# Mixture of experts in a two-layer decoder: routing and tiles in one stage, tiles of 256 tokens instead of 512

## The reference, cut to what matters

```
scores = sigmoid(x @ router_w.T) + routing_bias          # [4096, 8]
top 2 of the 8 experts, weights normalised by their sum
expert(x) = (silu(x @ wg.T) * (x @ wu.T)) @ wd.T         # wg, wu: [512, 256]; wd: [256, 512]
y = expert_shared(x) + sum over the 2 chosen e of weight_e * expert_e(x)
```

## Time and profile before

| | |
|---|---|
| time, median of 3 runs | 3147.19 us (3143.03 to 3158.15) |
| time of the profiled execution | 3143.8 us |
| its span | 3142.0 us |
| PE, PEld busy | 2614.6 us (83%), 2153.7 us (69%) |
| DVE, ACT, POOL busy | 1964.2 us (63%), 1431.5 us (46%), 1466.5 us (47%) |
| mean granted TensorE clock | 0.901 of 2.4 GHz |

### The profile page before, as it was taken

One profiled execution on the slowest core, in us unless ns is written; L12 is line 12 of the kernel. 1 busy time (PEld: TensorE's weight loads), 2 busy tenths in 40 slices (PEclk: granted clock), 3 DMA queues, 4 the chain that ended last, 5 costly groups with the idle time before them and its releaser, 6 DMA issues. The chain is left out here.

```text
span 3142.0 us, 67197 instructions
## 1 busy us (share of the span) xinstructions
PE 2614.6 (83%) x25004; PEld 2153.7 (69%) x25004; DVE 1964.2 (63%) x3461; ACT 1431.5 (46%) x2236; POOL 1466.5 (47%) x1604
## 2 busy tenths in 40 slices
PE   4999999994999964899999703888885799958998
PEld 3676667763666664788888603777775577747998
DVE  2676666673678714555555575887885377754554
ACT  2565555651566622344444302555552356632332
POOL 3565666653455315622222282444444477743333
PEclk7999999996999967999999956888897799989999
DMA  6565556624777624443434272000001777730111
GB/s 163 131 149 134 140 138 149 142 65 118 203 201 201 154 72 150 169 158 136 165 134 164 95 216 69 28 31 20 30 21 52 184 205 201 198 106 28 44 44 40
DMA packets 253341, 380.48 MB, mean 121 GB/s; under 512 B 53200, under 2 KB 190800, under 8 KB 246736
## 3 DMA queue, kind: packets, MB, share of 16 engines
q1 hardware_dynamic: 239328, 311.01, 37.3%
q0 software_dynamic: 10608, 65.55, 6.1%
q10 hardware_dynamic: 3200, 1.05, 0.2%
HBM read 242.80 MB, written 145.75 MB: 124 GB/s over the span
## 5 line engine op out<-in xcount | busy, mean ns | idle before, releaser
L1225 ACT ACTIVATE self_probs<-self_score_ps 128x768 f32<-128x768 f32 x256 | 207.6, 811 | 219.2 <-PE self_score_ps L1127 216.0
L1433 POOL TENSOR_SCALAR_AFFINE_SELECT self_probs<-self_probs 128x512 f32<-128x512 f32 x256 | 167.5, 655 | 217.5 <-ACT self_probs L1225 214.9
L1354 DVE TENSOR_REDUCE self_neg_max<-self_max_ps 128x2 f32<-128x256 f32 x256 | 108.2, 423 | 229.6 <-PE self_max_ps L1113 225.5
L1976 POOL TENSOR_TENSOR moee_w_lo<-moee_w_in,moee_w_hi 128x1536 fp32r<-128x1536 f32 x31 | 109.5, 3532 | 203.9 <-ACT moee_w_hi L1888 203.8
L672 DVE TENSOR_REDUCE cross_neg_max<-cross_max_ps 128x4 f32<-128x1024 f32 x128 | 155.9, 1222 | 67.0 <-PE cross_max_ps L461 65.8
L1912 DVE TENSOR_TENSOR moee_h<-moee_u_ps,moee_silu 128x512 f32<-128x512 f32 x124 | 85.5, 690 | 152.0 <-PE moee_u_ps L81 150.6
L1873 ACT ACTIVATE moee_h_hi<-moee_h 128x512 fp32r<-128x512 f32 x124 | 78.3, 632 | 221.5 <-DVE moee_h L1912 219.3
L1355 DVE TENSOR_REDUCE self_neg_max<-self_max_ps 128x2 f32<-128x512 f32 x256 | 174.6, 682 | 0.0
L1915 DVE TENSOR_TENSOR moee_h_lo<-moee_h,moee_h_hi 128x512 fp32r<-128x512 f32 x124 | 119.2, 961 | 86.5 <-ACT moee_h_hi L1873 76.0
L589 ACT ACTIVATE cross_probs<-cross_score_ps 128x1024 f32<-128x1024 f32 x128 | 131.1, 1024 | 89.4 <-PE cross_score_ps L483 89.2
L2823 POOL TENSOR_TENSOR ffn_g_lo<-ffn_g_full,ffn_g_hi 128x512 fp32r<-128x512 f32 x64 | 82.3, 1287 | 187.5 <-ACT ffn_g_hi L2747 187.5
(11 more groups left out here) (448 smaller groups left out, 9683.8 us busy)
## 6 DMA issues: line engine op xcount, KB each, us to landing
self_q<-self_q_split SPq DMA_DIRECT2D x48, 512.0 KB, 3.2
self_q_raw<-self_q SPq DMA_DIRECT2D x32, 768.0 KB, 7.9
cross_stacks<-cross_qk SPq DMA_DIRECT2D x64, 384.0 KB, 6.4
causal_stacks<-causal_qk SPq DMA_DIRECT2D x64, 384.0 KB, 6.7
moee_x_t<-x_tiles SPq DMA_DIRECT2D x31, 512.0 KB, 5.4
moe_y_tiles<-moee_y SPq DMA_DIRECT2D x31, 512.0 KB, 4.5
x_tiles<-zeros SPq DMA_DIRECT2D x16, 736.0 KB, 5.1
cross_qk<-cross_k_split SPq DMA_DIRECT2D x16, 512.0 KB, 3.9
```

The source lines that it names most:

```text
L1225: nc.scalar.activation(probs[g % 4][:, a, :, P:], score_ps[:, :, P:], ACT.Exp, scale=HD ** -0.5).then_inc(prob_ready, 1)
L1433: pool.affine_select(diagonal, diagonal, [[0, 2], [0, 2], [1, P]], ALU.is_ge, zero, base=0, channel_multiplier=-1).then_inc(prob_masked, 1)
L1976: pool.tensor_tensor(w_lo[p][:, 0:LO_POOL], w_in[:, 0:LO_POOL], w_hi[p][:, 0:LO_POOL].bitcast(F32), ALU.subtract).then_inc(wlo_ready, 1)
```

## The change

The stages route and expert_tiles become one stage (all names now `moee_`), and the tiles become smaller:

- TILE is 256. There are 16 shared and 39 routed tiles, 55 in all. Two blocks of hidden features make a pair, so that the ACT and DVE instructions on `silu` and `h` stay 512 columns wide; the matmuls of expand are 256 columns wide.
- The shared expert's weights are loaded and split once, while PE still transposes for the router (`scan`). Shared tiles take their tokens from `x_tok` in SBUF.
- Only the choice of experts stands ahead of the first tile on DVE (`choose`); the rest of the routing is put between the instructions of shared tiles 0, 1 and 2 (`weigh`, `count_chunks`, `start_experts`, `place_choices`, `name_tiles`), the two counting matmuls stand after the first tile's expand. The 64 scatters stand in one row on POOL.
- A routed tile's weights come in two indirect DMAs, 1 MB for gate and up (`in_raw`, asked for two tiles ahead) and 0.5 MB for down (`out_raw`, one tile ahead), each into two buffers. DVE writes the low part of half of the first, POOL that of the other half and of the whole second.
- Contract of a tile runs one tile later, between the expands of the next tile.

```diff
-TILE = 512
+TILE = 256
...
+            def rank_choices():
+                pe.wait_ge(both_ready, 1)
+                flat = both[:].rearrange("p c e -> p (c e)")
+                pe.matmul(prefix_ps, before, flat, start=True, stop=True)
+                pe.matmul(total_ps, ones, flat, start=True, stop=True).then_inc(prefix_done, 1)
...
             def body(st):
-                for f in range(WT):
+                for f in range(PAIRS):
+                    if f == 1 and st.has(1):
+                        transpose_x(st)
                     if st.has(0):
                         expand(st, f)
-                    if f == 0 and st.has(-1):
-                        contract(st, -1, WT - 1)
-                    if f > 0 and st.has(0):
-                        contract(st, 0, f - 1)
-                    if f == 0 and st.has(1):
-                        transpose_x(st)
+                    if f == 1 and shared(st) and st.at(0) == 0:
+                        rank_choices()
+                    if st.has(-1):
+                        contract(st, f)
...
+                for f in range(PAIRS):
+                    if f == 0 and fresh(st, 1):
+                        split_in(st)
...
+                    if f == 1 and fresh(st):
+                        split_out(st)
...
+                if fresh(st, 2):
+                    n = st.parity(2)
+                    if fresh(st):
+                        dve.wait_ge(out_loaded[buffer(st)], 16 * turn(st))
+                    dve.tensor_scalar(row[n][:], tile_expert[:, bass.ds(st.at(2), 1)], float(P), part_no,
                                       ALU.mult, ALU.add).then_inc(row_ready, 1)
-                for f in range(WT):
+                if fresh(st, 1):
+                    n = buffer(st, 1)
+                    dve.wait_ge(inhi_ready, sets(st, 1))
+                    dve.tensor_tensor(in_lo[n][:, IN_POOL:], in_raw[n][:, IN_POOL:], in_hi[n][:, IN_POOL:].bitcast(F32),
+                                      ALU.subtract).then_inc(inlo2_ready, 1)
+                for f in range(PAIRS):
+                    if f == 1 and st.has(1):
+                        dve.wait_ge(xhi_ready, st.done(1))
+                        if st.has(-1):
+                            dve.wait_ge(gu_done, 2 * PAIRS * st.done(-1))
+                        dve.tensor_tensor(x_lo[1 - p][:].rearrange("p k s -> p (k s)"), xT_ps[:],
+                                          x_hi[1 - p][:].bitcast(F32).rearrange("p k s -> p (k s)"),
+                                          ALU.subtract).then_inc(xlo_ready, 1)
                     if st.has(0):
...
+                    if f == 0 and st.has(-2):
+                        dve.wait_ge(down_done, PAIRS * st.done(-2))
+                        if st.has(-4):
+                            dve.wait_ge(stored[p], st.nth(-2) * 16)
+                        dve.tensor_copy(y[p][:].rearrange("p q d -> p (q d)"), y_ps[p][:]).then_inc(y_kept, 1)
+                    if shared(st) and st.has(0):
+                        if (st.at(0), f) == (0, 1):
+                            weigh()
+                            found["sums"] = count_chunks()
+                        if (st.at(0), f) == (1, 0):
+                            found["end"] = start_experts(found["sums"])
+                        if (st.at(0), f) == (1, 1):
+                            place_choices(found["sums"])
+                        if (st.at(0), f) == (2, 1):
+                            name_tiles(found["end"])
...
+            pool.wait_ge(inhi_ready, 1)
+            pool.tensor_tensor(in_lo[0][:, 0:IN_POOL], in_raw[0][:, 0:IN_POOL], in_hi[0][:, 0:IN_POOL].bitcast(F32),
+                               ALU.subtract).then_inc(inlo_ready, 1)
+            pool.wait_ge(outhi_ready, 1)
+            pool.tensor_tensor(out_lo[0][:], out_raw[0][:], out_hi[0][:].bitcast(F32),
+                               ALU.subtract).then_inc(outlo_ready, 1)
             pool.wait_ge(prefilled, B * 16)
-            n_scatter = -(-TOP * NT // (SHARED - 1))
+            for k in range(TOP):
+                pool.wait_ge(slot_ready, k + 1)
+                for c in range(NT):
+                    pool.indirect_dma_start(x_tiles, bass.IndirectOffsetOnAxis(ap=slot[k][:, c:c + 1], axis=0),
+                                            x_tok[:, c, :], None).then_inc(scattered, 16)
...
+                        pool.wait_ge(row_ready, sets(st, 2) - 1)
+                        pool.wait_ge(inlo_ready, sets(st))
+                        pool.wait_ge(inlo2_ready, sets(st))
+                    pool.wait_ge(outlo_ready, sets(st, -1))
                     pool.tensor_tensor(gate[:], part_no, part_no, ALU.add).then_inc(gate_set, 1)
-                    pool.indirect_dma_start(w_in[:], None, experts,
+                if fresh(st, 2):
+                    pool.indirect_dma_start(in_raw[buffer(st, 2)][:], None, experts_in,
+                                            bass.IndirectOffsetOnAxis(ap=row[st.parity(2)][:], axis=0)
+                                            ).then_inc(in_loaded[buffer(st, 2)], 16)
+                if fresh(st, 1):
...
+                    pool.indirect_dma_start(out_raw[n][:], None, experts_out,
                                             bass.IndirectOffsetOnAxis(ap=row[st.parity(1)][:], axis=0)
...
+                                            ).then_inc(out_loaded[n], 16)
+                    pool.wait_ge(inhi_ready, sets(st, 1))
+                    pool.tensor_tensor(in_lo[n][:, 0:IN_POOL], in_raw[n][:, 0:IN_POOL],
+                                       in_hi[n][:, 0:IN_POOL].bitcast(F32), ALU.subtract).then_inc(inlo_ready, 1)
+                if fresh(st):
+                    n = buffer(st)
+                    pool.wait_ge(outhi_ready, sets(st))
+                    pool.tensor_tensor(out_lo[n][:], out_raw[n][:], out_hi[n][:].bitcast(F32),
+                                       ALU.subtract).then_inc(outlo_ready, 1)
```

More of the change, by code:

```diff
@@ L1591, in _, with fresh, gate_cols, up_cols @@
+        def fresh(st, d=0):
+            return st.has(d) and not shared(st, d)
+        def gate_cols(t, k, f):
+            return t[:, k * FF + f * P:k * FF + (f + 1) * P]
+        def up_cols(t, k, f):
+            return t[:, (KT + k) * FF + f * P:(KT + k) * FF + (f + 1) * P]
         @block.sync
         def _(sp):
[L1593 to L1594 removed]
+            for dst, src in ((ident[:], consts["ident"]), (rw[:], router), (bias[:], router_bias.partition_broadcast(P)),
+                             (table[:], tables)):
@@ L1600, in _ @@
+            run(sp, body)
+            for p in range(2):
+                sp.wait_ge(stored[p], (ALL_TILES + 1 - p) // 2 * 16)
         @block.tensor
@@ new lines, in expand @@
+            def expand(st, f):
+                p, w, n = st.parity(0), buffer(st), st.at(0) * PAIRS + f
+                if f == 0:
+                    pe.wait_ge(xhi_ready, st.done(0))
+                    pe.wait_ge(xlo_ready, st.done(0))
+                    pe.wait_ge(inlo_ready, sets(st))
+                    pe.wait_ge(inlo2_ready, sets(st))
+                    if not st.has(-1):
+                        pe.wait_ge(scan_kept, SCANS)
+                if st.has(-1):
+                    pe.wait_ge(h_ready, n - 1)
+                for bank, cols in ((g_ps[f], gate_cols), (u_ps[f], up_cols)):
+                    for j in range(2):
+                        for k in range(KT):
+                            last = product3(pe, bank[:, j * TILE:(j + 1) * TILE],
+                                            (cols(in_hi[w], k, 2 * f + j), cols(in_lo[w], k, 2 * f + j)),
+                                            (x_hi[p][:, k, :], x_lo[p][:, k, :]), k == 0, k == KT - 1)
+                    last.then_inc(gu_done, 1)
```

584 lines of the change are left out of this document (275 added, 309 removed).

## The result

The changed kernel took **3184.98 us** (median of 3 runs, 3182.30 to 3189.64), the kernel before 3147.19: a ratio of 1.0115, 95% interval 1.0070 to 1.0159. It is slower, and the forecast of 3046 us, faster with a chance of 0.95, was wrong. The same program was run again on three other chips: on two it took 3097 and 3102 us, 1.3% and 1.2% less than the kernel before there, and on the third 3176 us, 1.0% more.

What follows compares the result with a forecast made beforehand. The prediction took the tiles as bound by PE, behind a start in which PE waits. 3143.8 - 50.1 - 33.5 - 19.9 + 3 - 0.5 = 3042.8, with 3.4 us for the median: 3046 us; forecast 3036 to 3062, range 3032 to 3088.

Steps and rivals of the forecast that it cites:

- The start: Before the first tile: first product at 1186.7 instead of 1220.18 us, since little waits behind `both`; 33.5 us less.
- PE's work and the stalls of the first tiles: Tiles: 9.02 us of PE each, 50.1 us less in all; first tiles' stalls 3.8 instead of 23.7 us, 19.9 less.
- The account of the losses before: First tiles of the kernel before: 23.7 us lost, ascribed to 12.6 us idle and 8.4 us of half clock.
- Scatters: ... Hidden: Shared tiles: 64 scatters take 83 us on POOL, over 107 us in, before the first routed load at 126; no cost.
- The loop of VectorE and GpSimd, "+3 us": Routed tiles: the DVE-POOL loop sums to 9.1 us against PE's 9.02; 0.08 us for 39 tiles, 3 us.
- rival 1: Routed tiles: the DVE-POOL loop sets the pace at 9.6 to 10.2 us, 3065 to 3088 us in all; chance 0.20.
- The bound of 10.0 us: Routed tiles: upper bound on the loop if POOL's load waits for DVE's own `in_lo` (1.2 us); 39 us more.
- The waits of over 3 us that I named as a sign: Routed part: PE waits over 3 us and a clock below 1.00 would show the forecast wrong.
- Rival 2, the loads: Routed tiles: the two weight loads need 9 instead of 7.3 us, loop 9.9 us, 35 us more, 3081 us; chance 0.10.
- Rivals 3 and 4: Routed loads one after another, 292 us more at worst, chance 0.03; expand at half the 512-column time, 3034 us, chance 0.07.
- forecast 503 us: All tiles: the last product comes about 503 us after the first.

Runs made afterwards that it cites:

- a1: The changed kernel itself, unedited, run again on another chip (chip 4): 3097.35 us, ratio 0.9868 to the kernel before.
- h1: f3 plus a row number in its own buffer for the w_out load, copied by GpSimd, on a chip with the stall: 3130.88 us, ratio 0.9952.
- f1: The changed kernel with in_lo of routed tiles computed wholly on VectorE instead of half on GpSimd: four executions of 3061, 3071, 3110 and 3113 us.
- f3: f1 plus row numbers of routed tiles computed once and copied per tile by GpSimd: 3063.33 us, ratio 0.9755 to the kernel before.

## Why the prediction was wrong

**The start**: right. 0.70 us from `both` to the first product, forecast 0.7 to 1.

**PE's work and the stalls of the first tiles**: right. In a1 the 16 shared tiles took 145.0 us from `x_lo` to `x_lo`, 9.06 each, with the routing between them; forecast 16 * 9.02 = 144.3 and 3.8 us of stalls. (The account of the losses before adds up to 12.6 + 8.4 = 21.0 of the 23.7 us; the rest it left open, and nothing hangs on it.)

**"Scatters: ... Hidden"**: this step failed, and it made the sign. It counted 83 us of issuing as work of GpSimd alone, because in the earlier trace rows they cost PE nothing; but there they go out ten to a tile. In a row, on the chips that stall, they stop the other engines after 10 to 12 us: +77 us (222.4 against 145.0 us for the shared tiles). Unshown is why: no row says what PE's "issue" waits for, and the cause stays open. Shown is when (eight profiles: from 9.7 to 12.2 us into an unbroken row, until 1 to 9 us behind the end of its last scatter, in h1, where loads are issued at once behind it, 13), that PE runs on in rows of five or six with pauses, that neither the bytes moved nor code fetching does it, and on which chips it was met: 5, 7, 11 and 15 (11 and 15 only in rows of twelve and ten), not 2, 4 and 6, where rows of 15 to 64 went by. I couldn't have read it in the trace before: at the end of a row of ten (1221.75 to 1234.38 us) PE is busy for the whole of 1231.5 to 1236.5. Which chip that trace is of isn't on record, so a row of ten may be harmless there or may never have met a stall. I could have seen that the change makes a state that this trace never shows. (The kernel before, too, took 3147.3 to 3152.0 us on the four chips with the stall and 3138.2 to 3142.0 on the three without; whether its rows of ten have part in that isn't shown.)

**The loop of VectorE and GpSimd, "+3 us"**: this step failed too, and by itself it puts the time outside the range, at 3097 and 3102 us on chips without the stall. The hold was right, its length wrong. I let `h_lo` go through 0.53 us behind `in_lo`; it goes through behind `out_lo`, which follows at once, another 2.4 us: 9.1 + 2.4 = 11.5 us. Measured: 9.4 to 12.6 us, 10.8 in the mean, so 38 * 1.8 = 68 us instead of 3. That is rival 1 (chance 0.20, priced at 9.6 to 10.2) beyond its upper bound. The bound of 10.0 us rested on another hold, of a load's issue by VectorE's `in_lo`: it exists, but in the changed kernel it made 15 of `out_raw`'s issues only 0.3 us longer (1.24 to 1.26 instead of 0.94). The waits of over 3 us that I named as a sign came, and with them the clock of 0.95.

**Rival 2, the loads**: in the changed kernel no pace-setter. But behind the loop lies the next one, through the landing of `out_raw` (f1, f3: 11 us), and it too closes only with a hold, of `row`, `gate` or a load's issue by VectorE's `in_lo`. Rivals 3 and 4 didn't come.

**Sum.** First to last product: forecast 503 us, a1 568.3 (loop +65), after 647.9 (loop +70, stall +77). Without the stall the rest of a1's span came out 12 us below the forecast, on a chip on which before, too, took 6 us less.

## What to carry to other kernels

When two engines hold each other, sum the loop with everything that the holder has queued behind its instruction, not with that instruction alone; and look for a second pace, into which one late instruction can tip the kernel (in f3 it came 1.1 us late and cost 2 us in every tile behind it). A stretch that the change makes longer than anything in the trace (here 64 DMA issues in a row instead of ten) is a bound that is unknown, even on an idle engine: break it up with waits on the work beside it. And measure on more than one chip before a result of one per cent is believed.

## What the hardware showed unasked

- On four chips of seven, an unbroken row of indirect DMA issues on GpSimd (one in 1.27 us) slows TensorE, ScalarE and VectorE after 9.7 to 12.2 us, TensorE down to one matmul in 1.6 us on average, the starts up to 4.2 us apart and mostly in steps of 0.70 us; with 64-byte rows as with 1-KB rows, in loops too. In rows of six with pauses of 1.3 us and more it doesn't come. What it is stays open.
- A VectorE subtraction of two SBUF operands (2.29 us) holds GpSimd's small copies (1.8 us instead of 0.2) and its DMA issues (2.79 us instead of 0.95) until it has ended; 36 such issues in h1.
- The same VectorE instruction is held through two GpSimd instructions back to back, 4.82 us instead of 0.69, while those with an operand in PSUM keep their 0.68.
- In all 19 profiles of the changed kernel and its variants the 114th indirect DMA that GpSimd issues starts 0.83 to 2.09 us behind the instruction before it, the other issues of `in_raw` 0.50 at most.
